# Gating in two expert layers: edges of the last node merged inside the window loop, two gate functions moved from GpSimd to ScalarE

## The reference

```python
h = (x_flat @ W_gat).reshape(M, 4, 4)            # M = 8192 nodes, 4 heads of 4
src, dst = edges plus one self loop per node
e = leaky_relu(a_src[src] + a_dst[dst], 0.2)
e_max = segment_max(e, dst);  ee = exp(e - e_max[dst])
alpha = ee / (segment_sum(ee, dst)[dst] + 1e-16)
agg = segment_sum(h[src] * alpha, dst).reshape(M, 16) + b_gat
scores = layernorm(agg, ln_gamma, ln_beta).reshape(M, 4, 4).mean(1)
topk_s, topk_i = top_k(scores, 2);  w = softmax(topk_s)
for ei in range(4):
    g = where(topk_i == ei, w, 0).sum(-1)
    out += g[..., None] * (gelu(x @ W1[ei] + b1[ei]) @ W2[ei] + b2[ei])
```

## Time and profile before

| | us |
|---|---|
| median of three runs | 4210.85 (4207.6 to 4214.59) |
| profiled execution, its time | 4212.08 |
| its span, first to last instruction | 4210.3 |
| busy PE / DVE / ACT / POOL in the span | 3549.8 / 3011.6 / 1491.1 / 1434.7 |
| experts and gates behind the histogram, layer 0 (L1694 to the last L1884) | 2093 to 2606 |
| the same, layer 1 | 3690 to 4202 |

### The profile page before, as it was taken

How to read it: one execution, slowest core, us unless ns; L and a number is a source line. 1 busy time by engine, 2 the same in 40 slices (tenths; PEclk the granted TensorE clock), 3 DMA queues, 4 the chain that set the end, 5 groups by cost and what they waited for, 6 DMA issues and landing times. The chain is left out here.

```text
span 4210.3 us, 51761 instructions
## 1 busy us (share of the span) xinstructions
PE 3549.8 (84%) x17914; PEld 2021.5 (48%) x17914; DVE 3011.6 (72%) x6268; ACT 1491.1 (35%) x2073; POOL 1434.7 (34%) x1016
## 2 busy tenths in 40 slices
PE   5999999999967987887799994685997878799996
PEld 2333333333325653555465652474753555565654
DVE  2676677667648887778988156867797779888257
ACT  2565555556543520122243420222530112233421
POOL 2776666667650000007730511000000006740520
PEclk9999999999986998888799997786999988899998
DMA  3000000000006300001131347126310001131247
GB/s 141 11 31 11 21 31 21 11 31 31 21 24 221 115 37 16 26 26 37 33 54 56 107 181 291 47 71 210 139 47 11 25 21 41 33 45 40 78 185 290
DMA packets 144857, 301.60 MB, mean 72 GB/s; under 512 B 20580, under 2 KB 103140, under 8 KB 139492
## 3 DMA queue, kind: packets, MB, share of 16 engines
q1 hardware_dynamic: 98212, 180.78, 12.0%
q10 hardware_dynamic: 25920, 94.38, 5.8%
q0 software_dynamic: 20480, 23.14, 3.6%
HBM read 183.42 MB, written 114.81 MB: 71 GB/s over the span
## 5 line engine op out<-in xcount | busy, mean ns | idle before, releaser
L1097 PE MATMUL l_pu<-l_tt,l_w 128*128 128x512 f32 x2048 | 1004.4, 616 | 34.7 <-ACT l_hid L1288 21.7
L1108 PE MATMUL l_pd<-l_w,l_hid 128*128 128x256 f32 x4096 | 968.8, 380 | 9.6 <-ACT l_hid L1288 9.6
L1108 PEld LDWEIGHTS l_pd<-l_w,l_hid 128*128 128x128 f32 x4096 | 782.2, 191 | 328.9 <-issue 246.8
L1288 ACT ACTIVATE l_hid<-l_pu,l_b 128x512 f32<-128x512 f32 x512 | 350.3, 687 | 1306.8 <-PE l_pu L1097 1298.1
L389 DVE TENSOR_TENSOR at_pr<-at_ps,at_decay 128x1024 f32<-128x1024 f32 x512 | 601.1, 1217 | 182.6 <-PE at_ps L503 181.5
L1042 POOL DMA_INDIRECT l_g<-hs_rows,l_i_src x336 | 391.6, 1165 | 905.1 <-DVE l_i_src L1658 803.3
L307 ACT ACTIVATE at_ab<-at_pr 128x1024 f32<-128x1024 f32 x512 | 537.1, 1055 | 436.3 <-DVE at_pr L389 400.4
L258 POOL TENSOR_TENSOR at_ab<-at_ab 128x1024 f32<-128x1024 f32 x256 | 600.9, 2372 | 180.6 <-ACT at_ab L307 180.6
L1097 PEld LDWEIGHTS l_pu<-l_tt,l_w 128*128 128x128 f32 x2048 | 400.2, 199 | 334.5 <-issue 312.8
L503 PE MATMUL at_ps<-at_qr,at_kr 32*128 32x512 f32 x2048 | 348.9, 644 | 14.5 <-issue 9.5
L522 PE MATMUL at_ps_av<-at_pr,at_v 128*32 128x512 f32 x2048 | 281.5, 612 | 7.3 <-ACT at_o L315 5.1
(11 more groups left out here) (341 smaller groups left out, 4189.0 us busy)
## 6 DMA issues: line engine op xcount, KB each, us to landing
ys<-l_yst ACTq DMA_DIRECT2D x112, 512.0 KB, 2.6
l_yb<-ys SPq DMA_DIRECT2D x28, 2048.0 KB, 9.9
l_tt<-tT ACTq DMA_DIRECT2D x36, 512.0 KB, 3.4
at_xt<-in_x SPq DMA_DIRECT2D x16, 1024.0 KB, 5.1
l_xt<-x SPq DMA_DIRECT2D x32, 512.0 KB, 4.1
tT<-l_xnT ACTq DMA_DIRECT2D x32, 512.0 KB, 4.5
l_xo<-x SPq DMA_DIRECT2D x28, 512.0 KB, 4.3
x<-at_xt SPq DMA_DIRECT2D x8, 1024.0 KB, 4.3
```

What stands on the lines that cost most here:

```text
L1097: ins = pe.matmul(ps_u[q % 2][:, :], w1[:, e, c, P * q:P * q + P], tt[:, s, c, :], start=(c == 0), stop=(c == KK - 1))
L1108: ins = pe.matmul(out, hid[:, k % 2, c, P * r:P * r + P], w2[:, k % GE, c, :], start=False, stop=(c == MB - 1), skip_group_check=True)
L1288: act.activation(hid[:, k % 2, q, :], ps_u[q % 2][:, :], ACT.Gelu, bias=b1[:, k % GE, q:q + 1]).then_inc(s_act, 1)
```

## The change

In neither layer is anything computed differently. (1) The initial state is the self loop alone: denominator 1, sums a copy of `l_hs`, no function on ACT. (2) The edges of the last node are merged inside the window loop: the exponents (7 instructions) behind the scan, the function on ACT at a new place `IN_CLAMPED = 32`, and the update (14 instructions) behind the sort, ahead of the wait for the gathered rows. (3) The merge's function on ACT moves from step 52 to 56. (4) `var ** -0.5` becomes a square root on ACT and a reciprocal on DVE, and the exponential of the softmax becomes ACT's. On ACT these two stand among the last experts: the square root after two of their steps, the exponential after three more.

```diff
-IN_MERGE = 52
+IN_CLAMPED = 32
+IN_MERGE = 56
...
         @block.gpsimd
-            pool.wait_ge(s_var, 1)
-            pool.tensor_tensor(rstd2, var, nhalf, ALU.pow).then_inc(s_rstd, 1)
-            pool.wait_ge(s_dif, 1)
-            pool.tensor_tensor(v2, euler, v1, ALU.pow).then_inc(s_ex, 1)
...
         @block.scalar
-            pre(6)
-            act.wait_ge(s_e0, 1)
-            act.activation(ye[:, :, :, :], ym[:, :, :, :], ACT.Exp).then_inc(s_p0, 1)
-            pre(4 * (PRE_PAIRS) + 4 - at[0])
+            pre(4 * PRE_PAIRS + 4 - at[0])
...
+                loop(IN_CLAMPED)
+                act.wait_ge(s_e0, m + 1)
+                act.sem_inc(s_go, 1)
+                act.activation(ye[:, :, :, :], ym[:, :, :, :], ACT.Exp).then_inc(s_p0, 1)
                 loop(IN_MERGE)
...
-            experts(4 * (PAIRS - PRE_PAIRS - LOOPED) + 4, PRE_PAIRS + LOOPED, PAIRS, LAST)
+            experts(2, PRE_PAIRS + LOOPED, PAIRS, LAST)
+            act.wait_ge(s_var, 1)
+            act.activation(deviation, var, ACT.Sqrt).then_inc(s_rstd, 1)
+            experts(3, PRE_PAIRS + LOOPED, PAIRS, LAST)
+            act.wait_ge(s_dif, 1)
+            act.activation(v2, v1, ACT.Exp).then_inc(s_ex, 1)
+            experts(4 * (PAIRS - PRE_PAIRS - LOOPED) - 1, PRE_PAIRS + LOOPED, PAIRS, LAST)
...
         @block.vector
-            then(dve.tensor_tensor(tm, el_, es, ALU.subtract))
-            then(dve.tensor_scalar(tm, tm, 0.0, None, ALU.max))
-            then(dve.tensor_tensor(tm, tm, over(cz[:, :], GH), ALU.mult))
-            then(dve.tensor_tensor(top[:, :, :], es, tm, ALU.add))
-            then(dve.tensor_tensor(ym[:, :, :, :], ym[:, :, :, :], top[:, :, :].unsqueeze(1).to_broadcast([P, 2, NT, GH]), ALU.subtract))
-            dve.tensor_scalar(ym[:, :, :, :], ym[:, :, :, :], 0.0, None, ALU.min).then_inc(s_e0, 1)
-            dve.wait_ge(s_p0, 1)
...
+            dve.memset(den, 1.0)
+            then(dve.tensor_copy(state[:, :, GH:SUMW], hs[:, :, 0:GF]))
...
                 dve.nop().then_inc(s_rout, 1)
 
+                then(dve.tensor_tensor(tm, of_last[:, :, :], top[:, :, :], ALU.subtract))
+                then(dve.tensor_scalar(tm, tm, 0.0, None, ALU.max))
+                then(dve.tensor_tensor(tm, tm, over(cz[:, :], GH), ALU.mult))
+                dve.tensor_scalar(ym[:, 0, :, :], tm, -1.0, None, ALU.mult)
+                then(dve.tensor_tensor(top[:, :, :], top[:, :, :], tm, ALU.add))
+                then(dve.tensor_tensor(ym[:, 1, :, :], of_last[:, :, :], top[:, :, :], ALU.subtract))
+                dve.tensor_scalar(ym[:, 1, :, :], ym[:, 1, :, :], 0.0, None, ALU.min).then_inc(s_e0, 1)
                 dve.wait_ge(s_slots, m + 2)
                 dve.sem_inc(s_go, 1)
                 sort()
+                dve.wait_ge(s_p0, m + 1)
+                dve.sem_inc(s_go, 1)
...
+                dve.memset(count[:, :], 0.0)
+                then(dve.memset(cz[:, :], 0.0))
+                then(dve.tensor_tensor(state[:, :, :], state[:, :, :], sum2[:, :, :], ALU.add))
                 for k in range(ABREAST):
                     dve.wait_ge(s_fnd[k], m * landed(NT, FOUND_GROUP, k) + landed(NT, FOUND_GROUP, k))
...
-            then(dve.memset(nhalf, -0.5))
-            then(dve.memset(euler, float(np.e)))
...
             dve.wait_ge(s_rstd, 1)
+            then(dve.reciprocal(rstd2, deviation))
             then(dve.tensor_tensor(acc, acc, over(rstd2, GF), ALU.mult))
```

More of the change, by code:

```diff
@@ L813, in ffn_layer @@
             top = sb("top", [P, NT, GH])
+            of_last = sb("of_last", [P, NT, GH])
             new = sb("new", [P, NT, GH])
@@ L847, in ffn_layer @@
         prod = pay[:, :, :].rearrange("p k j -> p (k j)")[:, 0:LOOK * NT].rearrange("p (j c) -> p j c", c=NT)
-        es, el_, tm = ym[:, 0, :, :], ym[:, 1, :, :], new[:, :, :]
+        tm = new[:, :, :]
         flat_rows = rows[:, :, :].rearrange("p j c -> p (j c)")
@@ L852, in ffn_layer @@
         t4, s4, beats, is1, is2 = (spare[:, NT * GE * k:NT * GE * k + NT * GE].rearrange("p (t f) -> p t f", f=GE) for k in range(5))
-        mean, var, rstd2, nhalf, c1, c2, best, second, v1, v2, euler = (
-            spare[:, NT * GE * 5 + NT * k:NT * GE * 5 + NT * k + NT] for k in range(11))
+        mean, var, rstd2, deviation, c1, c2, best, second, v1, v2 = (
+            spare[:, NT * GE * 5 + NT * k:NT * GE * 5 + NT * k + NT] for k in range(10))
         def bank(name):
@@ L1705, in _ @@
             dve.wait_ge(s_last, 16)
[L1706 to L1711, removed]
@@ L1728, in _ @@
-            then(ins)
-            then(dve.tensor_tensor(agg, agg, agg2, ALU.add))
+            den, den2 = state[:, :, 0:GH], sum2[:, :, 0:GH]
+            then(dve.tensor_tensor(top[:, :, :], hs[:, :, GF:HSW], ad[:, :, :], ALU.add))
+            leaky(top[:, :, :], top[:, :, :], tm)
+            then(dve.tensor_tensor(of_last[:, :, :], ad[:, :, :], last[:, GF:HSW].unsqueeze(1).to_broadcast([P, NT, GH]), ALU.add))
+            leaky(of_last[:, :, :], of_last[:, :, :], tm)
+            then(dve.tensor_scalar(cz[:, :], count[:, :], 1.0, None, ALU.min))
@@ L1800, in _ @@
                 sort()
+                dve.wait_ge(s_p0, m + 1)
+                dve.sem_inc(s_go, 1)
+                then(dve.tensor_tensor(ye[:, 1, :, :], ye[:, 1, :, :], over(count[:, :], GH), ALU.mult))
+                then(dve.tensor_tensor(den, den, ye[:, 0, :, :], ALU.mult))
+                for h in range(GH):
+                    cols = slice(GH + GE * h, GH + GE * h + GE)
+                    dve.tensor_tensor(state[:, :, cols], state[:, :, cols], ye[:, 0, :, h:h + 1].to_broadcast([P, NT, GE]), ALU.mult)
+                    ins = dve.tensor_tensor(sum2[:, :, cols], last[:, GE * h:GE * h + GE].unsqueeze(1).to_broadcast([P, NT, GE]),
+                                            ye[:, 1, :, h:h + 1].to_broadcast([P, NT, GE]), ALU.mult)
+                dve.tensor_copy(den2, ye[:, 1, :, :])
+                dve.memset(count[:, :], 0.0)
+                then(dve.memset(cz[:, :], 0.0))
+                then(dve.tensor_tensor(state[:, :, :], state[:, :, :], sum2[:, :, :], ALU.add))
                 for k in range(ABREAST):
```

## The result

The changed kernel takes 4236.89 us (median of 6 runs, 4230.22 to 4243.02), the kernel before 4210.75 us (6 runs, 4207.6 to 4215.63). The ratio is 1.0061, with a 95% interval of 1.0046 to 1.0075: it is slower, by about 26 us. The profiled execution of the changed kernel took 4241.68 us with a span of 4239.9 us, 29.6 us more than the span before.

A forecast was written before the change was run, and what follows sets the result against it. PE, busy 84% of the span, was taken as the bound, its last experts setting the sums' start. Late gates cost 10.9 us a layer, twice 21.8: 4210.9 + 21.8 = 4232.7, stated as 4231 for possible clock gains; range 4210 to 4242.

The forecast's parts named there:

- 10.9: First direct pair's second half: forecast delay in us per layer, with the 3.3 won and 3 lost contained.
- Minus 3.3 at the exchange: Exchange of lists in the loop: PE's 3.31 us wait for DVE's marks goes, saving 3.3 us.
- the clock's 1.9 us: First `up` after the exchange: a shorter wait might keep the clock up and win 1.9 us; kept for the range.
- Plus 3 for the tokens: Last experts' token loads, competing with SP's later first loads, come 0 to 5.9 us late; half taken, plus 3.
- 0 for the work in the loop: Exponents, update and ACT's exponential inside the window loop fit into existing waits, chiefly DVE's 70.33 us, and cost 0.
- 19.7 us at the merge: Merge: with its function four steps later on ACT, DVE waits 5.9 + 13.8 = 19.7 us for it.
- 1.28 us of table load behind the wait for the difference: Gates' exponential on ACT: 0.1 us of signal, 1.28 of table load and 0.25 of function follow the difference.
- Restart 3.7 and 2.3 us: PE after its wait for the sixth step's gelu: `up` takes 3.7 us and `down` some 2.3 us.
- The whole tail moves: After the first direct pair: DVE and PE are both late, so everything to the layer's end shifts by 10.9 us.
- the gates don't set the start: Rival, chance 0.12, faster: the tail makes up DVE's lateness, only the exchange's 3.3 us (5.2 with clock) remain; 4204 to 4200.
- are slow but cost nothing: Gates' two POOL powers, 10.79 and 10.72 us: they run while ACT and PE are busy with the loop's experts.
- each switch drains: Rival, chance 0.08, slower yet: three table switches on the path cost 4.1 us more a layer; 4241.

The follow-up runs named there:

- f1: The kernel before, unaltered, run and traced again: 4210.26 us, ratio 1.0003.
- f2: The changed kernel with IN_MERGE back at 52 instead of 56: 4226.67 us, ratio 1.0040 to the kernel before.
- e3: The changed kernel plus one unread power on POOL behind the variance: 4773.78 us on a slower chip, ratio 1.0046 to the kernel before.
- g1: Changed kernel plus an unread POOL power, square root ahead of the direct experts, exponential behind the fifth gelu: 4754.01 us on a slower chip, ratio 1.0003 to the kernel before.
- g3: The kernel before with only the merge moved as in the changed kernel, powers kept on POOL: 4754.15 us on a slower chip, ratio 1.0000.
- f4: Changed kernel plus unread POOL power, square root before direct experts, exponential after second gelu, exchange and later loop places six steps earlier: 4229.19 us, ratio 1.0048 to kernel before.
- e2: The kernel before with only the gates' square root and exponential on ACT, at the changed kernel's places: 4776.41 us on a slower chip, ratio 1.0051.
- e4: The changed kernel, unaltered, run again on a slower chip: 4778.17 us, ratio 1.0048 to the kernel before.

## Why the prediction held, and where it did not

The range (4210 to 4242) holds the 4236.9, and slower was right. The mechanism in the gates was right: a square root behind the first fill (it ends at 2457.58, said 2456.8), VectorE waiting 31.93 us for it (said: about 32), gates ready at 2476.00 (said 2476.8), PE standing 5.39 us (said: about 7) before the `up` at 2475.68, which takes 3.75 us at low clock, second half at 2482.31 (said 2482.4). But the count came 4.1 us later in that trace, so by the count the second half is 6.6 us late and not 10.9, and in layer 1 it is 4.6 (4097.49 less 3714.4, against 4069.02 less 3690.5). Against f1's layer 0 it would be 9.3. The prediction reached its 21.8 us from two layers; the layers give 11.9, and 17.7 come from stages that it took as unchanged. That the measured time lies only 6 us from the forecast is therefore luck in good part: what the layers lack, other stages made up for. The place and the kind of the loss in the gates are not luck. From PE's first `up` to the second half the prediction has 34.8 us (2482.4 less 2447.65), and the trace 34.2. Term by term:

- *Minus 3.3 at the exchange.* At a like clock it was 3.2 to 4.0, as forecast. In this trace it was 6.0, because the clock's 1.9 us, which I left out, came too, but not for the reason given: f1 has them with the wait, f2 lacks them in layer 1 without it.
- *Plus 3 for the tokens.* PE waited 8.56 us against 6.52: plus 2.0. f2, with the old IN_MERGE, has 7.2 and 6.4 us.
- *0 for the work in the loop.* Right: DVE waits 57.55 us for the rows instead of 70.33.
- *19.7 us at the merge.* 17.85.
- *1.28 us of table load behind the wait for the difference.* The load ran ahead of the wait; the sum there was 1.3 us too long, and DVE waited 0.38 us and not 1.7.
- *Restart 3.7 and 2.3 us.* 3.75 and 2.93. The 10.9 us are a slip of the sum: 2482.4 less 2471.64 is 10.8.
- *The whole tail moves.* Right: from the second half to the layer's last mark it is 148.0 us before and 147.7 after in layer 0, 141.3 and 142.4 in layer 1. Nothing is absorbed, so the rival "the gates don't set the start" is out.
- *The two powers "are slow but cost nothing", and nothing is paid for taking them away.* This is the step that failed. They cost nothing, but with them there the convolution's first power was on time. Without them DVE waits 4.2 us more for it (6.09 less 1.86), and with one power left in the gates (e3) it no longer does.
- *Stages without a changed line do not move.* The lists of layer 1 took 6.2 us more, nearly all of it in DVE's waits for small matmuls of PE, many of which grew from 2.41 to some 3.5 us. The two traces part at the first direct difference after the convolution, ACT's issue of two token loads, which took 1.95 us before and 1.48 after, so that PE's first `up` there came 0.4 us earlier against the marks; some 540 us behind the convolution the granted clock reads 0.87 and 0.70 in the same stretch (windows of before and after):

```profile
3386.97:3406.97 20.00, 18.55 (x88) 12.31 (x87) 19.97 (x76) 5.27 (x9) 0.00 (x0) 0.87 0.02 9
```

```profile
3404.71:3424.71 20.00, 17.10 (x120) 12.11 (x118) 19.97 (x56) 3.26 (x5) 0.00 (x0) 0.70 0.00 1
```

  What sets the time of that issue is open, and that it is the cause is argued, not shown: f1 has 1.78 us with lists of 843.5 as before, and g1 has the same 1.48 us and g3 1.94, whose lists, 1047.2 and 1048.2, don't follow it.
- *The first stage's 4.1 us* is no effect of the change: f2 to f4 have 2091.6 to 2093.7 us there, before and f1 2093.1 and 2090.6.

Of the rivals, "each switch drains" has the nearest number, 4241, and is nevertheless wrong. "ScalarE: Activation LUTs" of the Trainium skill (What ACT_TABLE_LOAD costs) adds 1.38 us of drain to each switch. The rows above have none: fill until 2456.01, load at 2456.03, square root at 2457.32, load at 2457.59, gelu at 2458.89. That this rival's number is the nearest is chance. g1 makes the same switches and keeps the time of the kernel before.

## What to carry to other kernels

A function moved to an engine that also feeds the bottleneck costs what its wait keeps from the instructions behind it. Place it where its operand is already there: the same two functions cost about 10 us a layer behind the second and the fifth gelu, when the exponential's operand hangs on a late square root, and nothing that could be measured when the square root goes ahead of the pair. A rare function taken off an engine can make that engine's next use of it, in another stage, a late one (4.2 us here); look for that use before counting the removal as free. And before a gain of a few us is put down to a cause, trace the unchanged kernel twice: here two traces of it differ by 2.7 us at one and the same mark.

## What I had not expected of the hardware

- The convolution's first power on POOL began 3.5 to 4.4 us after its operand, and DVE waited 5.2 to 6.1 us instead of 1.9, in the four kernels whose gates have no power on POOL (the changed kernel, e2, e4 and f2) and in none of the others. A pause alone does not do it: the gates' own first power was on time after 1386 and 1662 us. I had seen only the powers' own 10.6 us.
- The same program takes 4209 us on one chip and 4753 on two others. In layer 0's lists on one of these (e4) PE's matmuls of the histogram come singly in the stretch shown, 2.80 us from start to start, while POOL issues its gathers; windows and PE's timeline:

```profile
2000.00:2040.00 40.00, 2.97 (x14) 1.55 (x15) 0.00 (x0) 0.00 (x0) 30.25 (x33) 0.50 0.08 8
```

```profile
1987.51 0.21 PE L1159 MATMUL l_ph<-l_one_hi,l_one_lo 128*128 128x64 bf16 x1 [2.59 <-issue]
1990.31 0.21 PE L1159 MATMUL l_ph<-l_one_hi,l_one_lo 128*128 128x64 bf16 x1 [2.59 <-issue]
```

  On the chip of the result PE ran its expert steps without a gap beside such gathers (an `up` of four matmuls in 1.88 us at 1961.89). DVE stood 96.84 and 54.04 us in this stage of e4, with "remote" named as the releaser. Why PE issues so slowly there is open. The loop ends on other waits there too: in e4 DVE waits 83.69 us for ACT at the merge, where the changed kernel's first trace has 17.85. Whether that has the same cause is not shown.
